# Attention of a two-layer transformer rewritten: half-array score matmuls, stacks copied inside SBUF, an unrolled order by a table

## The chip, the cores and the metric

One core of one Trainium2 chip runs the whole kernel, in one launch. The metric is the device time in microseconds, from the first to the last instruction; a comparison takes the median of several executions.

## The reference

x has 32 batches of 256 rows with 256 features, and ctx has the same shape. The network is four residual steps, each on the layer norm of x:

```python
x = x + lora_attention(layernorm(x), ctx)     # layer 0: weights W + 2*A@B, 16 heads of 16
x = x + sqrt((n @ cos(theta'))**2 + (n @ sin(phi'))**2)     # n = layernorm(x)
x = x + rope_attention(layernorm(x), ctx)     # layer 1: q, k rotated by position, 16 heads of 16
x = x + quantised_ffn(layernorm(x))           # 256 -> 1024 -> gelu -> 256
# attention: softmax(q k^T / 4) v, heads joined, times Wo, plus bo
```

Queries come from x, keys and values from ctx. All is float32.

## The kernel before, in words

`transformer` (L1302) runs five blocks one after the other: `start` (loads x, which stays in SBUF, and its statistics), `attention` for layer 0, `cos_sin_ffn`, `attention` for layer 1, and the two quantised parts. Only `attention` and a little of `start` are touched by the change.

In `attention` each engine has its own program, and semaphores tie them. The work is done by batch. Float32 accuracy is kept by splitting a number into a rounded part (HI) and the rest (LO), both of the type float32r, and adding three products: hi*hi, hi*lo, lo*hi. For a batch:

- ScalarE makes xn (L456); PE transposes xn and ctx (L307); ScalarE and VectorE take the HI and LO parts of both (L481, L487, L542).
- PE projects q and k, 12 matmuls each (L315), and v, 12 more (L324). ScalarE adds the bias and takes the HI part (L445, L449), VectorE the LO part (L547, L552). In layer 1 q and k are first rotated: VectorE shuffles rows by 8 (L560) and multiplies by the sine (L562), GpSimd multiplies by the cosine and adds (L267, L270, L280, L283).
- The parts are stored in DRAM (L195) and come back as stacks (L199): for each head, 16 rows each of HI, LO and HI of q, and HI, HI and LO of k, beside rows of zeros up to row 96. Twelve DMAs of 128 KB do this for a batch, six for each half of the heads, all issued by SyncE.
- Scores: 32 matmuls of 96 rows (L418) into `s_bank`. VectorE takes the row maxima, 16 reductions of 128x512 (L610). The negated maxima are split (L568, L570), transposed by PE (L346), copied (L575) and moved by a DMA into rows 96 and 97 of the stack of q (L204), where the stack of k has ones.
- Transposed scores: 32 matmuls of 98 rows (L429) into `t_bank`, which so already hold the score minus the maximum. ScalarE takes the exponential, 16 times 128x512 (L475).
- 64 matmul instructions give the products with v (L339); a column of ones in `vext` (L616) gives the denominators. ScalarE copies them out (L496, L511). GpSimd stores them in DRAM (L255, L287), loads the denominators (L259), stores their inverses (L274) and loads them (L276), PE spreads them over the rows (L384), GpSimd loads the products (L291), VectorE multiplies (L653), the result is split (L508, L542) and projected (L324), and VectorE adds it to x (L665); GpSimd adds bo (L263).

The order is written out by hand: `step(i, q)` has 16 slots k. In one slot PE does the scores of slot k for batch i+1 and the transposed scores of slot k for batch i, and the other pieces stand at fixed k. Batch i+2 is being prepared meanwhile and batches i-1 and i-2 are being finished. Steps 5 to 28 run in a hardware loop of two steps (`drive`), the others are written out. The buffers `qhl` and `khl` are single, and the stacks are double. The second half of a batch's stacks waits for the transposed scores of the batch two before it, since it writes the same buffer.

Of the kernel before, what the change touches and what calls it, by code (L numbers as in the profile page):

```python
# [7 lines left out]
F32 = mybir.dt.float32  # L19
# [58 lines left out]
def attention(core, layer, w, x_res, stats, extent, consts, src, scratch):  # L78

# [11 lines left out]
    with ExitStack() as ctx:  # L91
# [6 lines left out]

        qst = [sb(f"qst{j}", [98, H, S], F32R) for j in range(2)]
        kst = [sb(f"kst{j}", [98, H, S], F32R) for j in range(2)]
        prob = [sb(f"prob{j}", [P, NT, 4, S]) for j in range(2)]
        vext = [sb(f"vext{j}", [P, NT, H, SLOT]) for j in range(2)]
        whl = {n: sb(f"w{n}", [P, 2, KT, D], F32R) for n in "qkvo"}
        ctx_in = sb("ctx_in", [P, NT, D])
        xn = sb("xn", [P, NT, D])
        xT = sb("xT", [P, 2, KT, S], F32R)
        cT = sb("cT", [P, 2, KT, S], F32R)
        qhl = sb("qhl", [P, 2, KT, S], F32R)  # L110
        khl = sb("khl", [P, 2, KT, S], F32R)
        osb = sb("osb", [P, 2, 2, S])
        yd = sb("yd", [P, KT, S])

        HI, LO = (1, 0) if rope else (0, 1)
        qf, kf = (hl[:, LO, :, :].bitcast(F32) for hl in (qhl, khl))
        yhl = xT
        negm = sb("negm", [P, 2, HT, NT])
        mhl = sb("mhl", [P, 2, 2, HT * NT], F32R)
        mT = sb("mT", [2 * HT * NT, 2, P], F32R)  # L120
        den = sb("den", [P, 32])
        rden = sb("rden", [P, 32])
        rhl = sb("rhl", [P, 2, 32], F32R)
        rin = sb("rin", [2 * H, S], F32R)

        nmr, rstd = stats[:, :, 0], stats[:, :, 1]
        bqk = sb("bqk", [P, 2, KT])
        bv = sb("bv", [P, D])
        bo = sb("bo", [P, D])
        bst = sb("bst", [P, NT, 6])  # L130
        mvt = sb("mvt", [P, NT, 2])

# [1257 lines left out]
```

## Time and profile before

| what | value |
|---|---|
| runs, median of 3 | 2484.71 us (2483.47 to 2512.54) |
| profiled execution, span from first to last instruction | 2491.9 us |
| PE, VectorE, ScalarE, GpSimd busy | 78%, 70%, 53%, 32% |
| granted PE clock, mean | 0.880 of full speed |

No time other than its span is given for the profiled execution. In the profile, PE is the matmul row of TensorE and PEld its weight loads, DVE is VectorE, ACT ScalarE, POOL GpSimd, SP SyncE; a q behind a name is that engine's queue of DMA issues. L610 is line 610 of the kernel before.

### The profile page before, as it was taken

What the parts mean: (1) busy time and instruction counts of PE and PEld (TensorE: products, weight loads), DVE (VectorE), ACT (ScalarE), POOL (GpSimd) and SP (SyncE); (2) the same over time, 40 slices, a digit from 0 to 9 for tenths busy, and PEclk for the clock granted to TensorE, in tenths of its full rate; (3) what the DMA queues carried; (4) which work ended last, traced back from release to release, by engine and by line L of the source; (5) the groups of instructions that cost most, each with busy time, mean ns of one, the idle gap of its engine ahead of it and who ended that gap; (6) DMA issues with size and microseconds to landing.
All of it is one profiled execution on the core that took longest, in us unless ns stands there. A gap on an engine that the chain in (4) does not pass through costs nothing. (4 is left out here: it accounts for less than half of the span.)

```text
span 2491.9 us, 47293 instructions
## 1 busy us (share of the span) xinstructions
PE 1955.9 (78%) x14240; PEld 1576.1 (63%) x14240; DVE 1747.3 (70%) x3674; ACT 1316.8 (53%) x2381; POOL 797.0 (32%) x866
## 2 busy tenths in 40 slices
PE   1689999999999679277788777887777775786687
PEld 0567777777777467255666666666666663665676
DVE  6567778877877378465667767767666665676788
ACT  0255666656655378144444444444444443786676
POOL 3012222222222200423333333333333332221787
PEclk9899999999999689578888888888888877898899
DMA  5576887888878100356665656666666661356565
GB/s 164 107 157 145 169 172 162 166 169 166 170 161 165 53 3 0 76 104 122 123 120 116 117 109 116 119 112 118 111 118 122 121 118 54 135 220 252 196 242 186
DMA packets 259781, 333.54 MB, mean 134 GB/s; under 512 B 29152, under 2 KB 237184, under 8 KB 251520
## 3 DMA queue, kind: packets, MB, share of 16 engines
q1 hardware_dynamic: 233088, 277.00, 49.4%
q0 software_dynamic: 26624, 55.67, 9.6%
q8 instruction: 37, 0.61, 0.1%
q14 instruction: 32, 0.26, 0.0%
HBM read 185.70 MB, written 144.70 MB: 133 GB/s over the span
## 5 line engine op out<-in xcount | busy, mean ns | idle before, releaser
L610 DVE TENSOR_REDUCE L_negm<-L_s_bank 128x2 f32<-128x512 f32 x1024 | 684.4, 684 | 363.2 <-PE L_s_bank L418 360.7
L475 ACT ACTIVATE L_prob<-L_t_bank 128x512 f32<-128x512 f32 x1024 | 598.9, 598 | 631.8 <-PE L_t_bank L429 625.7
L418 PE MATMUL L_s_bank<-L_kst,L_qst 96*128 96x256 f32 x2048 | 526.1, 343 | 236.5 <-DMA L_kst<-k_scratch 176.7
L418 PEld LDWEIGHTS L_s_bank<-L_kst,L_qst 96*128 96x128 f32 x2048 | 355.4, 216 | 363.0 <-issue 142.0
L429 PE MATMUL L_t_bank<-L_qst,L_kst 98*128 98x256 f32 x2048 | 460.6, 311 | 18.3 <-ACT L_prob L475 15.2
L429 PEld LDWEIGHTS L_t_bank<-L_qst,L_kst 98*128 98x128 f32 x2048 | 361.7, 217 | 33.3 <-ACT L_prob L475 30.0
L339 PE MATMUL L_o_bank<-L_prob,L_vext 128*32 128x256 f32 x4096 | 301.1, 415 | 2.7 <-ACT L_prob L475 2.7
L1289 PE MATMUL G_acc<-G_w_out,G_hhl 128*128 128x256 f32 x1024 | 140.4, 291 | 59.4 <-DVE G_hhl L1259 59.1
L259 POOL DMA_DIRECT2D L_den<-o_scratch x64 | 35.5, 554 | 452.2 <-DMA o_scratch<-L_osb 452.2
L1289 PEld LDWEIGHTS G_acc<-G_w_out,G_hhl 128*128 128x128 f32 x1024 | 127.9, 192 | 72.1 <-DVE G_hhl L1259 37.5
L339 PEld LDWEIGHTS L_o_bank<-L_prob,L_vext 128*32 128x32 f32 x4096 | 112.5, 115 | 92.6 <-issue 18.8
L324 PE MATMUL L_m<-L_wo,L_xT 128*128 128x256 f32 x768 | 133.7, 336 | 45.0 <-DVE L_xT L542 44.9
L1219 POOL TENSOR_SCALAR G_hs<-G_hq,G_winv 128x512 f32<-128x512 f32 x128 | 152.4, 1208 | 40.8 <-issue 23.2
L324 PEld LDWEIGHTS L_m<-L_wo,L_xT 128*128 128x128 f32 x768 | 120.8, 237 | 56.2 <-DVE L_xT L542 30.9
L255 POOL DMA_DIRECT2D o_scratch<-L_osb x64 | 48.0, 751 | 301.4 <-ACT L_osb L511 301.4
L1002 PE MATMUL G_hb<-G_xT,G_w_in 128*128 128x512 f32 x512 | 127.1, 401 | 12.0 <-DVE G_xT L1112 11.2
L291 POOL DMA_DIRECT2D L_yd<-o_scratch x128 | 77.9, 614 | 140.3 <-DVE L_xT L542 130.0
L1002 PEld LDWEIGHTS G_hb<-G_xT,G_w_in 128*128 128x128 f32 x512 | 94.9, 190 | 38.0 <-ACT G_hid L1044 14.2
L1107 DVE TENSOR_REDUCE G_hmax<-G_hid 128x512 f32 (+1 forms) x128 | 84.8, 682 | 45.3 <-ACT G_hid L1044 45.3
L315 PE MATMUL L_m<-L_xT,L_wq 128*128 128x256 f32 x768 | 115.5, 304 | 1.1 <-DVE L_xT L542 1.1
L324 PE MATMUL L_m<-L_wv,L_cT 128*128 128x256 f32 x768 | 110.9, 298 | 5.9 <-ACT L_khl L445 4.1
L315 PEld LDWEIGHTS L_m<-L_xT,L_wq 128*128 128x128 f32 x768 | 108.0, 213 | 3.6 <-DVE L_xT L542 1.9
(172 smaller groups left out, 3257.2 us busy)
## 6 DMA issues: line engine op xcount, KB each, us to landing
L_qst<-q_scratch SPq DMA_DIRECT2D x384, 128.0 KB, 5.0
L_kst<-k_scratch SPq DMA_DIRECT2D x384, 128.0 KB, 6.4
q_scratch<-L_qhl SPq DMA_DIRECT2D x64, 512.0 KB, 3.0
k_scratch<-L_khl SPq DMA_DIRECT2D x64, 512.0 KB, 3.2
o_scratch<-L_osb POOLq DMA_DIRECT2D x128, 256.0 KB, 4.8
hidden_scratch<-G_hid SPq DMA_DIRECT2D x32, 1024.0 KB, 3.9
G_hid<-hidden_scratch SPq DMA_DIRECT2D x32, 1024.0 KB, 7.4
L_ctx_in<-in_ctx SPq DMA_DIRECT2D x64, 256.0 KB, 3.2
```

The costliest lines, as they stand in the source:

```text
L291: pool.dma_start(yd[:, t, :], o_dram[1 - q, t].rearrange("g (s r) q -> (g s) r q", r=SLOT)[:, 0:HD, :]).then_inc(sem["y_load"], 16)
L315: mm = pe.matmul(dst[:, f, :], wt[:, cw, k, P * f:P * (f + 1)], act[:, ca, k, :], start=j == 0, stop=j == len(group) - 1)
L324: mm = pe.matmul(dst[:, t, :], act[:, ca, k, P * t:P * (t + 1)], wt[:, cw, k, :], start=j == 0, stop=j == len(group) - 1)
L339: mm = pe.matmul(o_bank[g // 2][SLOT * s:SLOT * (s + 1), g % 2, :], vext[q][:, kt, 4 * g + s, :], prob[g % 2][:, kt, s, :], start=kt == 0, ...
L418: mm = pe.matmul(s_bank[k % 2][:, j, :], qst[1 - q][0:96, h, P * qt:P * (qt + 1)], kst[1 - q][0:96, h, :], start=True, stop=True)
L429: mm = pe.matmul(t_bank[k % 2][:, j, :], kst[q][0:98, h, P * kt:P * (kt + 1)], qst[q][0:98, h, :], start=True, stop=True)
L475: act.activation(prob[g % 2][:, k % 2, 2 * (k // 2 % 2):2 * (k // 2 % 2) + 2, :], t_bank[k % 2][:, :, :], ACT.Exp, scale=HD ** -0.5).then_ ...
L610: dve.tensor_reduce(negm[:, t, 2 * pair:2 * pair + 2, qt], s_bank[k % 2][:, :, :], AX.X, ALU.max, negate=True).then_inc(sem["dve_s"], 1)
L1002: ins = pe.matmul(hb[f % 4][:, :], w_in[:, k, P * f:P * (f + 1)], xT[q][:, c, k, :], start=j == 0, stop=j == len(group) - 1)
L1107: dve.tensor_reduce(hmax[:, bass.ds(FT * i + f, 1)], hid[q][:, f, :], AX.X, ALU.max, apply_absolute_value=True).then_inc(sem["dve_h"], 1)
L1219: pool.tensor_scalar(hs[f % 4][:, :], hq[f % 4][:, :], -MAGIC, winv[:, f:f + 1], ALU.add, ALU.mult).then_inc(sem["pool_hs"], 1)
L1289: ins = pe.matmul(acc[q][t][:, 0:D], hhl[f % 4][:, c, P * t:P * (t + 1)], w_out[:, f, :], start=f == 0 and c == 0, stop=f == FT - 1 and c ...
```

## The change

`attention` is written anew; the other three computing blocks stay.

- **Stacks.** They are copied by DMA from `qhl` and `khl` inside SBUF, not by way of DRAM: again 12 DMAs of 128 KB for a batch, in rows of 2 KB where the loads before had 1 KB. The columns of Wq and Wk are reordered on the host so that the two halves of the heads lie on even and odd partitions. The half h of batch n lies on partitions 64u to 64u+47, with u = n%2 xor h, and the maxima and ones on the two rows after that, so scores have 48 rows and transposed scores 50. In a slot the four matmuls alternate between the two halves of the array.
- **Context.** It arrives transposed. Layer 0 splits it on GpSimd and stores the parts in DRAM (512 KB a batch), and layer 1 loads them.
- **Biases.** bo + bv@Wo is computed once and comes into the output projection as one more matmul of each row tile. The bias of v, the bias additions on GpSimd and the widening products of PE go.
- **After the products.** The two groups of heads go one after the other through one PSUM tile `eo`, with 17 columns a head. ScalarE copies each out. SyncE gathers denominators (2 DMAs), merges rows (4), stores inverses (2) and loads them spread over 128 rows (1). GpSimd multiplies and takes LO.
- **Rotation.** In layer 1 four DMAs inside SBUF (two each for q and k) swap the halves, and GpSimd does all six products and sums. VectorE has none.
- **Splits.** GpSimd takes all LO parts of q, k, y and, in layer 0, of ctx, and in layer 0 the HI parts too; ScalarE takes the HI parts of layer 1. GpSimd also makes xn. All DMAs of attention are now SyncE's; GpSimd issues none.
- **Maxima.** Their split is on GpSimd in layer 1 and stays on VectorE in layer 0.
- **Order.** A table `PLACE` gives each piece a batch offset and a slot for each layer, the same in all engines, and `HELD` names whom a PSUM bank must have been read by. All steps are written out: 39 for layer 0 (offsets 4 to -3) and 43 for layer 1 (4 to -7), with no hardware loop.
- The memsets of the stacks and the mask `bmask` go.

The diff, cut to its core:

```diff
-        qst = [sb(f"qst{j}", [98, H, S], F32R) for j in range(2)]
+        qst = [sb(f"qst{j}", [P, HJ, KT, S], F32R) for j in range(2)]
...
-            with eng.Fori(2, (B - 4) // 2) as r:
-                step(2 * r + 1, 1)
-                step(2 * r + 2, 0)
+        def drive(step):
+            for i in range(start_at, end_at):
+                step(i)
...
+            def stack(n, h):
+                u = n % 2 ^ h
+                for st, hl, parts in ((kst, khl, (0, 0, 1)), (qst, qhl, (0, 1, 0))):
+                    for c, part in enumerate(parts):
+                        row = 64 * u + HD * c
+                        sp.dma_start(st[n % 2][row:row + HD, :, :, :].bitcast(F32),
+                                     hl[n % NQ][h::2, part, :, :].bitcast(F32)).then_inc(sem[f"stack{h}"], 16)
...
+                    for n in due("sti0", i, k):
+                        sp.wait_ge(sem["pool_k"], n + 1)
+                        sp.wait_ge(sem["pool_q"], n + 1)
+                        after(sp, sem["pe_t"], 16 * (n - 2) + 8)
+                        after(sp, sem["stack0"], 96 * n)
+                        stack(n, 0)
+                    for n in due("sti1", i, k):
+                        after(sp, sem["pe_t"], 16 * (n - 1))
+                        after(sp, sem["stack1"], 96 * n)
+                        stack(n, 1)
...
+            def high(n, x, hl, f):
+                pool.wait_ge(sem[f"act_{x}"], n + 1)
+                for h in range(2):
+                    after(pool, sem[f"stack{h}"], 96 * (n - NQ + 1))
+                pool.tensor_copy(hl[n % NQ][:, 0, :, :], f[:, :, :]).then_inc(sem[f"high_{x}"], 1)
...
+                        for n in due(f"ms{h}", i, k) if rope else ():
+                            pool.wait_ge(sem["dve_s"], 16 * n + 8 * (h + 1))
+                            after(pool, sem["pe_mT"], 2 * (n - 1) + h + 1)
+                            pool.tensor_copy(mhl[:, h, 0, :], negm[:, h, :]).then_inc(sem["m_split"], 1)
...
+                    first = scores(i + 1, k) if on(i + 1) else iter(())
+                    second = scores_T(i, k) if on(i) else iter(())
+                    for _ in range(KT):
+                        next(first, None)
+                        next(second, None)
```

NQ is 1. In both layers the HI and LO parts of batch n+1 can be written only after both stack copies of batch n have landed.

## Rows read from the trace of the kernel before

**Rows 1.** Windows by stage (start:end, length, busy by engine, PEclk, DMA share, GB/s)
```profile
43.00:867.60 824.60, 731.71 (x6032) 580.00 (x6032) 595.90 (x1298) 449.68 (x867) 212.29 (x294) 0.93 0.73 149
999.30:2109.00 1109.70, 832.88 (x6016) 669.60 (x6016) 737.56 (x1486) 493.32 (x930) 392.89 (x422) 0.82 0.58 111
...
300.00:700.00 400.00, 383.06 (x3327) 305.17 (x3329) 319.63 (x706) 243.64 (x476) 104.69 (x159) 0.98 0.82 167
1200.00:2000.00 800.00, 634.36 (x4651) 510.77 (x4651) 555.24 (x1135) 377.89 (x715) 284.58 (x319) 0.84 0.62 116
```
**Rows 2.** One line, L189, 300:700 and then 1200:2000: the context load, once a batch
```profile
L189 SPq DMA_DIRECT2D L_ctx_in<-in_ctx x18: 402/403/407, 312.4 to 697.6; - x18
...
L189 SPq DMA_DIRECT2D L_ctx_in<-in_ctx x24: 400/403/446, 1221.4 to 1968.7; - x24
```
**Rows 3.** Waits, 1200:1800 (us in total, times, longest)
```profile
POOL L_den L259 <- DMA o_scratch<-L_osb: 166.9, 19, 9.7
...
PE L_s_bank L418 <- DMA L_kst<-k_scratch: 78.4, 19, 5.3
```
**Rows 4.** Groups of instructions, 100:800 (layer 0)
```profile
L610 DVE TENSOR_REDUCE L_negm<-L_s_bank 128x2 f32<-128x512 f32 x485 | 321.5, 683 | 105.6 <-PE L_s_bank L418 105.4
L475 ACT ACTIVATE L_prob<-L_t_bank 128x512 f32<-128x512 f32 x479 | 279.5, 599 | 229.0 <-PE L_t_bank L429 228.0
...
L449 ACT ACTIVATE L_khl<-L_m,L_bqk 128x256 fp32r<-128x256 f32 x60 | 25.0, 473 | 0.0
...
L542 DVE TENSOR_TENSOR L_xT<-L_m,L_xT 128x512 fp32r<-128x512 f32 x30 | 20.4, 680 | 0.0
...
L665 DVE TENSOR_TENSOR x_res<-L_m,x_res 128x512 f32 (+1 forms) x27 | 18.7, 691 | 2.2 <-issue 0.4
...
L575 DVE CAST L_mT<-L_m 32x128 fp32r<-32x128 f32 x61 | 16.7, 274 | 23.9 <-PE L_m L346 23.9
...
L568 DVE CAST L_mhl<-L_negm 128x16 fp32r<-128x16 f32 x60 | 10.4, 174 | 0.2
```
**Rows 5.** Groups of instructions, 1100:2060 (layer 1)
```profile
L263 POOL TENSOR_TENSOR x_res<-x_res,L_bo 128x256 f32 (+1 forms) x58 | 41.6, 745 | 0.5
...
L283 POOL TENSOR_TENSOR L_khl<-L_khl,L_rr 128x512 f32<-128x512 f32 x29 | 37.0, 1275 | 4.2 <-POOL L_khl L280 3.8
...
L499 ACT ACTIVATE L_khl<-L_khl 128x512 fp32r<-128x512 f32 x29 | 18.3, 630 | 47.8 <-POOL L_khl L283 47.8
```
**Rows 6.** Timeline of 420 to 425: projection, score matmuls and products with v at full clock
```profile
421.65 1.49 PEld L315 LDWEIGHTS L_m<-L_xT,L_wq 128*128 128x128 f32 x12
...
423.31 0.31 PEld L429 LDWEIGHTS L_t_bank<-L_qst,L_kst 98*128 98x128 f32 x2
423.55 0.31 PEld L418 LDWEIGHTS L_s_bank<-L_kst,L_qst 96*128 96x128 f32 x2
423.79 0.31 PEld L429 LDWEIGHTS L_t_bank<-L_qst,L_kst 98*128 98x128 f32 x2
...
424.24 1.07 PE L339 MATMUL L_o_bank<-L_prob,L_vext 128*32 128x256 f32 x16
425.24 0.50 PE L418 MATMUL L_s_bank<-L_kst,L_qst 96*128 96x256 f32 x2
```
**Rows 7.** DMA issues (KB each, median us from issue to landing)
```profile
L_qst<-q_scratch SPq DMA_DIRECT2D x384, 128.0 KB, 5.0
L_kst<-k_scratch SPq DMA_DIRECT2D x384, 128.0 KB, 6.4
```
**Rows 8.** Timeline, 78 to 90: the first stacks of layer 0, with nothing beside them
```profile
82.08 1.25 SPq L199 DMA_DIRECT2D L_kst<-k_scratch  x3
...
88.40 0.80 PE L418 MATMUL L_s_bank<-L_kst,L_qst 96*128 96x256 f32 x2 [8.39 <-DMA L_kst<-k_scratch]
```
**Rows 9.** Windows, 80:90, the same stretch (columns as in rows 1)
```profile
80.00:90.00 10.00, 1.61 (x8) 1.60 (x8) 0.77 (x2) 0.00 (x0) 0.00 (x0) 0.50 1.12 164
```
**Rows 10.** Timelines, 1014 to 1060: casts on VectorE beside work on GpSimd
```profile
1018.10 3.09 DVE L535 CAST L_wo<-L_prob 128x512 fp32r<-128x512 f32 x1
...
1059.95 1.26 POOL L270 TENSOR_TENSOR L_qhl<-L_qhl,L_rr 128x512 f32<-128x512 f32 x1
...
1059.98 1.27 DVE L568 CAST L_mhl<-L_negm 128x16 fp32r<-128x16 f32 x1
```

More of the change, by code:

```diff
@@ L111, in attention @@
[L111 to L120, printed above, removed]
+        NQ = 1
+        qhl = [sb(f"qhl{j}", [P, 2, KT, S], F32R) for j in range(NQ)]
+        khl = [sb(f"khl{j}", [P, 2, KT, S], F32R) for j in range(NQ)]
@@ new lines, in attention, with on, due @@
+        block = ctx.enter_context(nc.Block())
+        place = PLACE[layer]
+        start_at, end_at = lo - max(a for a, _ in place.values()), hi - min(a for a, _ in place.values())
+        def drive(step):
+            for i in range(start_at, end_at):
+                step(i)
+        def on(n):
+            return lo <= n < hi
+        def due(op, i, k):
+            ahead, slot = place[op]
+            return [i + ahead] if slot == k and on(i + ahead) else []
+        biases = 16 * (4 if rope else 3)
@@ new lines, in scores @@
+            def scores(n, k):
+                h, j, qt = k // 8, k % 8 // 2, k % 2
+                u = n % 2 ^ h
+                if k % 8 == 0:
+                    pe.wait_ge(sem[f"stack{h}"], 96 * (n + 1))
+                after(pe, sem["dve_s"], 16 * n + k - 1)
+                rows = slice(64 * u, 64 * u + ROWS)
+                for t in range(KT):
+                    mm = pe.matmul(s_bank[k % 2][:, t, :], qst[n % 2][rows, j, t, P * qt:P * (qt + 1)], kst[n % 2][rows, j, t, :],
+                                   start=True, stop=True)
+                    if t == KT - 1:
+                        mm.then_inc(sem["pe_s"], 1)
+                    yield
@@ new lines, in scores_T @@
+            def scores_T(n, k):
+                h, j, kt = k // 8, k % 8 // 2, k % 2
+                u = n % 2 ^ h
+                if n == lo and k == 0:
+                    pe.wait_ge(sem["ones0"], 64)
+                if k % 8 == 0:
+                    pe.wait_ge(sem[f"m_load{h}"], 16 * (n + 1))
+                after(pe, sem["act_p"], 16 * n + k - 1)
+                rows = slice(64 * u, 64 * u + ROWS + 2)
+                for t in range(KT):
+                    mm = pe.matmul(t_bank[k % 2][:, t, :], kst[n % 2][rows, j, t, P * kt:P * (kt + 1)], qst[n % 2][rows, j, t, :],
+                                   start=True, stop=True)
+                    if t == KT - 1:
+                        mm.then_inc(sem["pe_t"], 1)
+                    yield
@@ L435, in _ @@
+            drive(step)
         @block.scalar
@@ L1336, in shape_constants @@
     f = np.float32
-    head = np.arange(P) // HD
-    bmask = np.zeros((2 * H, KT, P), f)
-    for t in range(KT):
-        for part in range(2):
-            bmask[part * H + HT * t + head, t, np.arange(P)] = 1
     inv_freq = f(1.0) / np.power(f(10000.0), np.arange(0, HD, 2, dtype=f) / f(HD)).astype(f)
```

886 lines of the change are left out of this document (420 added, 466 removed), and 24 rows, old and new, of tables (HELD, PLACE).

## The prediction

> **What bounds the kernel now.** I read the windows by stage first, then the interval from batch to batch, then the waits, then the groups of instructions. Attention takes 824.6 us in layer 0 and 1109.7 us in layer 1 of the 2491.9 us [rows 1]; the rest isn't touched. The context load comes once a batch. In layer 0 it came 18 times from 312.4 to 697.6 us, so 385.2/17 = 22.66 us a batch; in layer 1, 24 times from 1221.4 to 1968.7, 747.3/23 = 32.49 us a batch [rows 2]. So 32 batches make 725 us and 1040 us, and 99.6 and 69.9 us are left for filling and draining the two layers.
>
> In layer 0 PE is busy in 383 of 400 us at a clock of 0.98 [rows 1]: it is PE's layer. The DMA engines are at 0.82 there. In layer 1 PE is busy in 634 of 800 us at 0.84, and what ends its longest idle stretch in each batch is the stack of k, 78.4 us in 19 waits, up to 5.3 us [rows 3]. Layer 1 is bound by a chain: rotation, split, store, stack, with GpSimd in the middle of it and blocked in its order by the load of denominators (166.9 us in 19 waits [rows 3]).
>
> **The change part by part, for one batch.**
>
> *PE.* A pair of score matmuls starts every 0.24 us (423.31, 423.55, 423.79), so a slot of four costs 0.48 us and 16 slots 7.7 us [rows 6]. The new order alternates the two halves of the array, in 48 and 50 rows. No row here shows two such matmuls at once. If they overlap fully a slot costs 0.24 us, 3.9 us a batch; if not, 7.7 us as now. The only matmuls side by side in this trace are those of 32 columns: 16 instructions with v in 1.07 us [rows 6], where their own passes one behind the other would take several times that. I take 4.5 us. The rest of PE: four projections at 1.49 us, 6.0; two bias matmuls at 0.12, 0.25; four groups with v at 1.0, 4.0; transposes of xn and maxima about 0.8. The context's transposes and the widening go, about 1.1 us. Sum 15.6 us at full clock, 18.8 without overlap.
>
> The Trainium skill, "TensorEngine Tiling (Array Packing)", section Key Properties, says that tiles work independently but that "Changing tiling mode (not just tile) drains the TensorE". The first half speaks for the 3.9 us, the second against this change, which goes from half-array to whole-array work and back at nearly every piece. The trace has such a change: the products with v began at 424.24 and the next score matmul at 425.24 [rows 6], 1.00 us where two rounds of four fill about 0.85, so at most 0.15 us a change. With two changes in each of 12 slots that is up to 3.6 us, and PE would need 19.2 us instead of 15.6; without the rule 15.6.
>
> *VectorE.* 16 reductions at 0.683 = 10.9; LO of xT 0.68; sum with x 0.69; two copies of maxima 0.55 [rows 4]; statistics, inverse and their kin 1.3. Layer 0 adds the four small splits at 0.174, 0.7 [rows 4], layer 1 the two extents, 1.3. Sum 14.9 in layer 0 and 15.5 in layer 1, from 18.1 (0.80 of 22.66) and 22.5 (0.694 of 32.49) [rows 1, 2].
>
> A cast between SBUF tiles on VectorE takes 0.174 us alone [rows 4] and took 1.27 us while GpSimd ran a sum that ended with it, and a 128x512 cast took 3.09 us beside memsets [rows 10]. In layer 1 that cast goes to GpSimd and can no longer be held. In layer 0 it stays, twice a batch, and GpSimd will be busy for 60% of the time, so it costs 2 x 0.6 x about 0.6 = 0.7 us more, between 0 and 2.2. It delays the maxima, which have slots to spare, so I put 0.5 us of it on the interval.
>
> *ScalarE.* 16 exponentials at 0.599 = 9.6; q and k 4 x 0.473 = 1.9 [rows 4]; xT, v and two copies of eo 4 x 0.6 = 2.4. Layer 0: 13.9. Layer 1 adds three HI copies at 0.63 [rows 5]: 15.8.
>
> *GpSimd.* A sum or product of 128x512 costs 1.275 us, of 128x256 0.745 [rows 5]. A cast of 128x512 on GpSimd has no row; its bounds are 0.6, what ScalarE needs [rows 5], and 1.275; I take 1.0, nearer to GpSimd's own. Layer 0: five products at 1.275, four casts at 1.0, xn 1.2, sum 11.6. Layer 1: ten at 1.275, xn 1.2, four small splits of maxima at 0.2 to 0.4, sum 15.2. It waits in order for the gathered denominators only once a batch, at a place where the table gives them two steps.
>
> *SyncE and the DMAs.* 25 issues in layer 0 and 28 in layer 1, at 0.43 us most, 11 to 13 us. Bytes for a batch fall from about 3.7 MB (0.82 of 22.66 us = 18.6 us of all engines [rows 1, 2]) to 2.7 and 2.9 MB: 1.5 stacks, 0.25 or 0.5 context, 0.5 stored or 0.5 rotated, 0.13 merged, 0.25 inverses. At the same rate that is 13.6 and 14.6 us.
>
> *The chain that decides.* Every engine now needs 14 to 16 us, and a loop needs more. The parts of batch n+1 may be written only when both stacks of batch n have landed, the second stack may be issued only when the transposed scores of batch n-2 are through, and the first stack of n+1 must have landed at the start of the next step. So the interval is at least second stack + splits + first stack. A stack is six DMAs. In the trace three issued from 82.08 on let PE go at 88.40, 6.3 us [rows 8], in a stretch with the engines full at 164 GB/s [rows 9]; single ones land after 5.0 and 6.4 us [rows 7]. 768 KB at 164 GB/s is 4.7 us, and with 2 us of fixed latency 6.7; rows of 2 KB and no DRAM may make it 5, a last landing behind other traffic 8.6 (2.2 to issue and 6.4). I take 6.5. The splits in layer 0 are four instructions of GpSimd in a row, 4.6 us, with handoffs 5.5; in layer 1 two HI copies on ScalarE and two of 1.275 us behind them, with GpSimd at other work for three quarters of the time: 6.5. Loop: 18.5 and 19.5 us. For slots in which two engines wait for each other in turn (now too VectorE idles 105 us of 700 for PE [rows 4]) I add 1 us: **19.5 us in layer 0, 20.5 us in layer 1.**
>
> *Fill and drain.* Layer 0: 17 us to the split weights (now 24; the memsets go, beside which a cast took up to 3.09 us [rows 10]), 21 to the first scores, 13 for the step of scores alone, 31 x 19.5 = 604.5, 11 for the last exponentials, 20 to drain. Sum 686.5. Layer 1: 14 + 28 (the rotation is longer) + 13 + 31 x 20.5 = 635.5 + 11 + 22 = 723.5. The offset of -7 costs nothing: late steps hold only short work. Straight-line code instead of a loop: the loop has no visible cost and so I take 0, with -3 to +15 us in all as bounds, since 82 steps of instructions must be fetched once.
>
> *Sum.* 824.6 - 686.5 = 138.1 and 1109.7 - 723.5 = 386.2; together 524.3. 2491.9 - 524.3 = 1967.6 against the profiled span; the median of the runs is 0.9971 of it, so **1962 us**.
>
> **The rivals.**
>
> A, *PE is the bound again.* Without overlap between the halves PE needs 18.8 us, with 0.15 us at each of 24 changes of shape [rows 6] 3.6 more, 22.4, and any clock under 1 on top. Layer 0 at 22.5 and layer 1 at 23: 31 x 3 + 31 x 2.5 = 170 more, 2132 us. For it: the clock is 0.82 in layer 1 where PE is busy in 79% [rows 1], and the new kernel has PE at about 80%. Against it: with the halves overlapped 15.6/0.84 = 18.6 is still under the loop.
>
> B, *the loop is shorter.* Stacks in 5 us give 15.5 us, and the engines' 16 us with the same 1 to 1.5 on top bound it: 17 and 18. 31 x 2.5 x 2 = 155 less, 1807 us. For it: half the packets. Against it: all six copies still land on 48 partitions.
>
> C, *slower than before.* The copies inside SBUF are slow, and through the single `qhl` and `khl` the interval pays each of them twice. It decides from 523/62 = 8.4 us a batch, which is 4.2 us more for each stack, 10.7 us. At 12 us the interval is 2 x 12 + 5.5 = 29.5 in both: 31 x (10 + 9) = 589 more, 2551 us. For it: the only copy inside SBUF now, the one of maxima, is 16 KB, and single stack DMAs have 128 KB. Against it: 128 KB is landed in 5.0 to 6.4 us now, with DRAM on one side and a fuller queue [rows 7].
>
> D, *the gain is eaten elsewhere and nothing changes.* It needs the price of C at 8.4 us by chance, or SyncE's one order of 28 issues blocking itself as GpSimd's did. 2470 us.
>
> **How the numbers follow.** Forecast 0.57, A 0.17, B 0.11, C 0.11, D 0.04. The likeliest gives 1962 us. Its own range is 1900 to 2040, an interval shorter or longer by 1.2 us. The range of 8 in 10 takes in the near half of B and most of A: 1860 to 2180. About 2% is what a measurement of this kernel can tell from no change. Faster by over 2% hold the forecast, A and B, 0.85; within it D, 0.04; slower C, 0.11.
>
> **What would show it.** In the profile after: the 1024 reductions of VectorE with starts 19 to 21 us apart from batch to batch; in a slot, weight loads of the two kinds of scores side by side and slots of 0.24 to 0.3 us where nothing waits; stack DMAs landing in 4 to 6 us; GpSimd's LO of q and k ending just before SyncE issues the first stack; PE's longest wait in each step being a stack, at slot 0 or 8. GpSimd at 60% in layer 0 and 75% in layer 1. The prediction is wrong if four score matmuls still take 0.48 us and PE is busy over 90% (A), if the interval is set by VectorE with no wait for a stack (B), or if a stack needs over 10 us (C).

## The result and the profile after

| | before | after |
|---|---|---|
| median of the runs | 2488.2 us | 2364.4 us (2362.1 to 2366.3, 4 runs) |
| ratio after / before | 1 | 0.948 [0.945, 0.952] |
| span of the profiled execution | 2491.9 us | 2364.4 us |
| attention, layer 0 and layer 1 | 824.6 and 1109.7 us | 895.7 and 909.7 us |
| interval per batch, layer 0 and 1 | 22.66 and 32.49 us | 25.93 and 25.97 us |

The kernel gained 5.2%, some 124 us where 524 were forecast. Layer 1 gained 200 us; layer 0, of which 138 us were expected, lost 71. First the windows of the kernel after: the two layers whole, then the steady part of layer 0 (columns as in [rows 1]).

```profile
43.00:938.70 895.70, 693.13 (x5908) 475.76 (x5908) 454.25 (x947) 406.52 (x771) 313.15 (x361) 0.81 0.57 103
1070.40:1980.10 909.70, 707.25 (x5892) 499.07 (x5892) 464.12 (x877) 450.16 (x865) 462.53 (x521) 0.79 0.65 111
...
300.00:700.00 400.00, 311.79 (x2795) 212.86 (x2791) 209.65 (x441) 190.42 (x363) 145.79 (x166) 0.83 0.61 109
```

In that steady part PE was busy in 383 us at a clock of 0.98 before [rows 1]; now it is 312 us at 0.83. No engine and not the DMA (0.82 before, 0.61 now) is near full in it. The interval per batch, here and for every run below, is read from the issue of the spread of the inverses (`rb`), once a batch. Its rows from the middle of the two layers:

```profile
L255 SPq DMA_DIRECT2D L_rb<-r_scratch x23: 670/672/677, 223.8 to 794.2; - x23
L255 SPq DMA_DIRECT2D L_rb<-r_scratch x26: 651/672/928, 1176.4 to 1825.6; - x26
```

570.4/22 = 25.93 us, 649.2/25 = 25.97 us. The waits of the two layers (us in total, times, longest), of 300:800 and of 1200:1800:

```profile
POOL L_yT L334 <- DMA L_rb<-r_scratch: 211.5, 19, 12.8
...
ACT L_osb L552 <- POOL L_yT L334: 112.1, 19, 7.7
PE L_eo L522 <- ACT L_osb L552: 106.7, 19, 7.4
...
POOL L_khl L311 <- DMA L_qst<-L_qhl: 53.5, 19, 4.0
...
POOL L_qr L319 <- DMA L_qr<-L_qf: 143.1, 23, 7.7
POOL L_kf L319 <- DMA L_kr<-L_kf: 72.1, 23, 4.9
...
PE L_s_bank L438 <- DMA L_qst<-L_qhl: 44.6, 23, 2.9
PE L_misc L471 <- POOL L_mhl L378: 40.7, 23, 3.0
```

The first four are layer 0: PE waits not for a stack but for ScalarE's copy of `eo`, ScalarE for GpSimd's product, GpSimd for the spread. The last four are layer 1: GpSimd's two longest waits are for the rotated copies, and PE waits for a stack and for the maxima's split. The timeline of one batch of layer 0 shows the first ring (start, length; in brackets the idle time ahead and what ended it):

```profile
417.56 0.57 SPq L228 DMA_DIRECT2D L_den<-L_osb  x1
419.33 1.91 SPq L217 DMA_DIRECT2D L_kst<-L_khl  x3
...
421.10 0.34 DVE L642 RECIPROCAL L_rden<-L_den 128x32 f32<-128x32 f32 x1
421.28 1.89 SPq L217 DMA_DIRECT2D L_qst<-L_qhl  x3
423.27 1.14 SPq L251 DMA_DIRECT2D r_scratch<-L_rden  x2
...
425.69 3.84 SPq L246 DMA_DIRECT2D L_osb<-L_osb  x4
429.63 0.68 SPq L255 DMA_DIRECT2D L_rb<-r_scratch  x1
430.40 1.88 SPq L217 DMA_DIRECT2D L_kst<-L_khl  x3
...
437.44 1.26 POOL L334 TENSOR_TENSOR L_yT<-L_osb,L_rb 128x512 f32<-128x512 f32 x1 [12.43 <-DMA L_rb<-r_scratch]
438.79 0.60 ACT L552 ACTIVATE L_osb<-L_eo 128x512 f32<-128x512 f32 x1 [7.38 <-POOL L_yT L334]
...
439.53 1.91 PE L522 MATMUL L_eo<-L_prob,L_vext 128*17 128x256 f32 x16 [7.11 <-ACT L_osb L552]
...
440.78 0.61 POOL L311 CAST L_khl<-L_kf 128x512 fp32r<-128x512 f32 x1 [2.08 <-DMA L_qst<-L_qhl]
```

The denominators leave at 417.56 and are inverted at 421.10; the inverses are stored only at 423.27, 1.8 us after they are ready, because a stack's six issues stand ahead in SyncE's order; the spread goes out at 429.63, behind four merges, and GpSimd's wait for it ends 7.8 us later, beside the next stack. Only then may GpSimd multiply and ScalarE copy the next half into the single `osb`, for which PE waits. The stack issued from 430.40 on is whole only when GpSimd can begin the next splits, at 440.78, 10.4 us later. All 25 issues of a batch of layer 0 share SyncE's one order.

The terms that had been forecast stand in the groups of layer 0 (300:700), the DMA issues, and one slot at full clock:

```profile
L622 DVE TENSOR_REDUCE L_negm<-L_s_bank 128x2 f32<-128x512 f32 x244 | 160.4, 683 | 185.0 <-PE L_s_bank L438 183.1
...
L311 POOL CAST L_qhl<-L_qf 128x512 fp32r<-128x512 f32 x15 | 9.2, 613 | 0.0
```
```profile
L_kst<-L_khl SPq DMA_DIRECT2D x384, 128.0 KB, 4.6
L_qst<-L_qhl SPq DMA_DIRECT2D x384, 128.0 KB, 5.3
...
L_qr<-L_qf SPq DMA_DIRECT2D x64, 128.0 KB, 4.8
L_kr<-L_kf SPq DMA_DIRECT2D x64, 128.0 KB, 6.8
```
```profile
406.98 0.28 PE L438 MATMUL L_s_bank<-L_kst,L_qst 48*128 48x256 f32 x1
...
406.98 0.28 PE L454 MATMUL L_t_bank<-L_qst,L_kst 50*128 50x256 f32 x1
...
407.21 0.28 PE L438 MATMUL L_s_bank<-L_kst,L_qst 48*128 48x256 f32 x1
```

Both kinds of score matmuls start at the same hundredth of a microsecond, and two pairs, which make a slot, take 0.23 us (406.98 to 407.21). That is the price where slots follow each other. Many stand between pieces of whole-array work, as here in the kernel after, and then, for comparison, the start of the score matmuls behind the projection of [rows 6] in the kernel before:

```profile
417.70 0.98 PE L427 MATMUL L_misc<-L_wv,L_cT 128*128 128x256 f32 x6
...
418.61 0.38 PE L438 MATMUL L_s_bank<-L_kst,L_qst 48*128 48x256 f32 x1
...
419.04 0.98 PE L427 MATMUL L_misc<-L_wv,L_cT 128*128 128x256 f32 x6
```
```profile
423.07 0.31 PEld L418 LDWEIGHTS L_s_bank<-L_kst,L_qst 96*128 96x128 f32 x2
```

Six whole-array matmuls and one slot of two pairs take 1.34 us (417.70 to 419.04), where eight passes at 0.115 us would take 0.92: each of the two changes between whole-array and half-array work costs 0.2 us. The matmul records of 300:700 hold some 20 such changes a batch, 4 us by that price (an estimate). In the kernel before, the twelve weight loads from 421.65 on and the first of the scores at 423.07 are 0.118 us apart, so that change cost nothing.

### The profile page after: what moved, and what is told of

Read it like the earlier page. It is cut to its first block and busy times, and to the rows that moved or that the text cites. A ratio compares the mean times of both kernels' runs of the same rounds, so it can differ in the third digit from the quotient of the medians.

```text
span 2364.4 us, 41257 instructions
## 1 busy us (share of the span) xinstructions
PE 1792.0 (76%) x13992; PEld 1301.9 (55%) x13992; DVE 1332.9 (56%) x2715; ACT 1230.9 (52%) x2221; POOL 969.2 (41%) x1032
## 5 line engine op out<-in xcount | busy, mean ns | idle before, releaser
L438 PE MATMUL L_s_bank<-L_kst,L_qst 48*128 48x256 f32 x2048 | 495.0, 354 | 74.5 <-DMA L_qst<-L_qhl 65.9
L454 PE MATMUL L_t_bank<-L_qst,L_kst 50*128 50x256 f32 x2048 | 485.1, 352 | 43.4 <-DMA L_qst<-L_mT 33.6
L438 PEld LDWEIGHTS L_s_bank<-L_kst,L_qst 48*128 48x128 f32 x2048 | 336.6, 217 | 264.6 <-issue 95.6
L522 PE MATMUL L_eo<-L_prob,L_vext 128*17 128x256 f32 x4096 | 351.4, 480 | 164.5 <-ACT L_osb L552 164.5
L454 PEld LDWEIGHTS L_t_bank<-L_qst,L_kst 50*128 50x128 f32 x2048 | 334.6, 218 | 61.0 <-DMA L_qst<-L_mT 42.8
L427 PE MATMUL L_misc<-L_wo,L_yhl 128*128 128x256 f32 x768 | 135.4, 322 | 0.0
L420 PE MATMUL L_misc<-L_xT,L_wq 128*128 128x256 f32 x768 | 130.5, 309 | 2.1 <-DVE L_xT L637 2.1
L427 PE MATMUL L_misc<-L_wv,L_cT 128*128 128x256 f32 x768 | 130.9, 311 | 0.9 <-ACT L_qf L538 0.9
L420 PE MATMUL L_misc<-L_cT,L_wk 128*128 128x256 f32 x768 | 122.2, 305 | 4.3 <-POOL L_cT L348 4.3
L427 PEld LDWEIGHTS L_misc<-L_wo,L_yhl 128*128 128x128 f32 x768 | 124.6, 233 | 0.0
```

Source lines behind the costliest of these rows:

```text
L420: mm = pe.matmul(bank[x][:, f, :], whl[x][:, cw, k, P * f:P * (f + 1)], act[:, ca, k, :], start=j == 0, stop=j == 5)
L427: mm = pe.matmul(bank[x][:, t, :], act[:, ca, k, P * t:P * (t + 1)], whl[x][:, cw, k, :], start=j == 0 and x != "o", stop=j == 5)
L438: mm = pe.matmul(s_bank[k % 2][:, t, :], qst[n % 2][rows, j, t, P * qt:P * (qt + 1)], kst[n % 2][rows, j, t, :], start=True, stop=True)
L454: mm = pe.matmul(t_bank[k % 2][:, t, :], kst[n % 2][rows, j, t, P * kt:P * (kt + 1)], qst[n % 2][rows, j, t, :], start=True, stop=True)
L522: mm = pe.matmul(eo[SLOT * j:SLOT * j + VS, t, :], vext[n % 3][:, kt, VS * head:VS * (head + 1)], prob[h][:, kt, j, t, :], start=kt == 0, ...
```

## The experiments

Intervals in us per batch, each read over the first 28 of a layer's 31 intervals; the last three, where the layer drains, are mostly 15 to 21 us and are left out. The ratio is to the kernel before, with its 95% interval.

| run | median us | ratio | layer 0 | layer 1 |
|---|---|---|---|---|
| after | 2364.4 | 0.948 [0.945, 0.952] | 26.0 | 26.0 |
| f1_osb2 | 2317.3 | 0.929 [0.926, 0.932] | 24.6 | 26.3 |
| f2_nq2 | 2357.6 | 0.947 [0.944, 0.950] | 25.7 | 26.2 |
| g1_osb2_nq2 | 2236.2 | 0.898 [0.895, 0.900] | 21.9 | 26.0 |
| f3_order0 | 2419.6 | 0.972 [0.969, 0.975] | 27.7 | 25.9 |
| h2_both_order0 | 2419.4 | 0.970 [0.966, 0.974] | 28.1 | 26.1 |
| h1_cut_loops | 2227.4 | 0.893 [0.890, 0.896] | 21.7 | 26.2 |
| h3_no_merge | 2306.5 | 0.926 [0.922, 0.930] | 24.5 | 25.6 |
| g2_act_queue | 2429.1 | 0.976 [0.974, 0.979] | 24.5 | 29.3 |
| g3_osb2_nq2_actq | 2403.3 | 0.964 [0.961, 0.967] | 24.0 | 29.2 |
| i1_pool_merge | 2384.6 | 0.958 [0.954, 0.963] | 20.6 | 32.2 |
| f4_ms_dve | 2360.7 | 0.947 [0.945, 0.950] | 25.8 | 26.3 |
| i2_bufs_ms_dve | 2227.4 | 0.896 [0.892, 0.901] | 21.6 | 26.1 |
| g4_apart | 2361.9 | 0.949 [0.945, 0.953] | 25.8 | 26.1 |
| i3_small_third | 2255.2 | 0.907 [0.904, 0.911] | 25.2 | 23.0 |
| j2_bufs_small_third | 2120.3 | 0.850 [0.847, 0.853] | 20.9 | 23.2 |
| j1_best | 2213.7 | 0.889 [0.885, 0.892] | 20.5 | 26.4 |

Kernels that have the same code in a layer differ by up to 0.4 us there, so less than that shows nothing. Some of the recorded texts below put the kernel with both buffers at 24.2 to 25 us in layer 1, and i3 at 3.5 us less than the kernel after: those were read over other stretches, some with draining batches in them. Read alike, layer 1 stands at 26.3 us with `osb` doubled (28 intervals from 1133.9 to 1869.9) and at 26.0 with both buffers (1058.8 to 1786.1).

### The two single buffers

```diff
-        osb = sb("osb", [P, 2, KT, S])
+        osbs = [sb(f"osb{j}", [P, 2, KT, S]) for j in range(2)]   # f1, g1: osbs[n % 2]
...
-                            after(act, sem["pool_y"], n)
+                            after(act, sem["pool_y"], n - 1)
...
-        NQ = 1
+        NQ = 1 if rope else 2                                     # f2, g1
```

f1_osb2:

> osb is doubled in both layers, so the copy of eo for batch n+1 no longer waits for the product of batch n; nothing else moves. Theory T1 (in layer 0 the loop through the single osb binds: copy of eo, denominators, inverses, their spreading, product, next copy): PE's 7 us stall before the products with v goes, and the interval of layer 0 falls from 25.9 to 20 to 22 us, layer 1 stays: 2190 to 2260 us. Theory T2 (the loop of the prediction, through the single qhl and khl, binds, now with SyncE's issues in it): the stall moves to the stacks and the interval stays at 25 to 26 us: 2340 to 2365 us.

f2_nq2:

> qhl and khl are doubled in layer 0 alone. T1: no change, 2355 to 2370 us. T2: the interval of layer 0 falls by the splits and the landing that leave the loop, 3 us or more: 2270 us or less.

g1_osb2_nq2:

> osb doubled in both layers and qhl/khl doubled in layer 0, that is the two buffers of the two earlier runs together. Theory of two loops (copy of eo, inverses, product; and splits, first stack, second stack, each closed by one single buffer): alone the doubled osb left 24.6 us a batch of layer 0 and the doubled qhl/khl 25.7; together neither loop is left there, the batch falls to what the engines and issues want, 19 to 21 us, so 2317 - 32 x 4.6 = about 2170 us (2120 to 2220). Rival, that SyncE's one order of issues with its waits carries the interval whatever the buffers: 24 to 24.6 us a batch, 2300 to 2320 us. Layer 1 at 26.0 in both.

Alone the doubled `osb` brought 47 us, and the doubled parts 7, with layer 0's interval at 25.7; together they brought 128. In f1 PE's waits for the copy of `eo` went, but the ring of splits and stacks held. One lap of it, from f1's timelines of SyncE, PE and GpSimd:

```profile
404.95 1.90 SPq L218 DMA_DIRECT2D L_kst<-L_khl  x3
...
413.35 0.38 PE L439 MATMUL L_s_bank<-L_kst,L_qst 48*128 48x256 f32 x1 [0.54 <-DMA L_qst<-L_qhl]
...
414.66 1.87 SPq L218 DMA_DIRECT2D L_kst<-L_khl  x3
...
426.20 0.61 POOL L312 CAST L_khl<-L_kf 128x512 fp32r<-128x512 f32 x1 [3.48 <-DMA L_qst<-L_qhl]
...
429.90 1.88 SPq L218 DMA_DIRECT2D L_kst<-L_khl  x3
```

The first stack is issued from 404.95 on, and PE waits for it until 413.35, 8.4 us. The second is issued 9.7 us after the first, and GpSimd's splits wait for it until 426.20, 11.5 us. The splits take 3.7 us, and the next first stack leaves at 429.90: 9.7 + 11.5 + 3.7 = 24.9 us in this lap, for a mean of 24.6. So two rings of nearly one length lay beside each other in layer 0, and only cutting both pays: 26.0 to 21.9 us. Of the 19 to 21 us expected g1 kept 0.9 more than the upper end, and its time is 16 us outside the range given. Layer 1 stayed at 26 us, as expected.

### Where the issues stand in SyncE's order

```diff
-     "sti0": (3, 5), "mg": (0, 9), "rs": (0, 6), "rb": (0, 10)    # layer 0: f3, and h2 on g1
+     "sti0": (3, 6), "mg": (0, 5), "rs": (0, 5), "rb": (0, 6)
...
-     "ym": (-1, 8)                                                # layer 0: h1 on g1
+     "ym": (-2, 2)
...
-     "kr": (1, 3)                                                 # layer 1: h1 on g1
+     "kr": (2, 14)
```

f3_order0:

> Layer 0's table only: merging, storing and spreading of the inverses are issued by SyncE before the first stack of the next batch, not behind it. T1: the product starts 6 to 8 us earlier after the copy of eo, and the interval falls to about 20 us until the stack, issued later, binds: 2170 to 2250 us. T2: the first stack comes later, and the interval grows or stays: 2360 us or more.

h2_both_order0:

> The kernel with both buffers, and layer 0's table as in the earlier run of another order (merges, store of the inverses and spread ahead of the first stack), which alone cost 55 us. Theory: alone it delayed the splits' ring, which was closed by the single qhl/khl; with two of each it cuts the ring through the spread instead (store, merges and spread no longer wait for the stack), so the same edit now saves: 19 to 20.5 us a batch for 21.4, 2160 to 2215 us. Rival, that an earlier place of these issues is simply bad (they block SyncE until the inverses are ready): slower than 2236 here too, by 20 to 60 us.

h1_cut_loops:

> The kernel with both buffers (2236 us), and one step moved in each layer. Layer 0 (21.4 us a batch there): GpSimd's product with the spread inverses goes behind the splits of k and q, so the splits, and with them the first stack and all that SyncE issues behind it, no longer wait for the spread (spread 7.5 us, product and splits 5.0, stack 3.8, store, merges and the next spread 5.1 = 21.4). Theory that this ring through SyncE's and GpSimd's orders sets the interval: 17 to 19.5 us a batch, 32 x 3 = about 100 us less. Layer 1 (24.2 us there): the rotated copies of k are issued ahead of the spread and the load of c, 1.4 to 2 us earlier in the ring rotated copies, rotation, splits, first stack, rotated copies: 22.5 us a batch, 40 to 60 us less. So about 2090 us (2050 to 2140). Rival, DMA or TensorE near their bound (TensorE 16 to 17 us, DMA 14): layer 0 stays at 20.5 or above and the total at 2180 or more.

Putting the inverses ahead of the first stack cost 55 us alone and 183 us where both buffers are doubled, against the 20 to 75 us of gain that I expected there. The waits of h2_both_order0, layer 0 (265:800), and its timeline say why:

```profile
PE L_s_bank L439 <- DMA L_qst<-L_qhl: 134.4, 20, 9.4
```
```profile
414.22 0.60 ACT L553 ACTIVATE L_osb<-L_eo 128x512 f32<-128x512 f32 x1 [0.39 <-PE L_eo L523]
...
420.97 0.65 SPq L256 DMA_DIRECT2D L_rb<-r_scratch  x1
421.79 1.86 SPq L218 DMA_DIRECT2D L_kst<-L_khl  x3
```

The next stack is issued only behind the store and the spread, which wait for the present batch's copy, which waits for its matmuls: scores, products, inverses and the next stack are in one line, and PE stands for it up to 9.4 us a batch. An issue that waits for the end of the present batch must not stand ahead of one that feeds the next.

h1 moved GpSimd's product behind the splits. The splits no longer waited for the spread, but the interval stayed at 21.7 us; in layer 1, where the rotated copies of k were issued earlier, it stayed at 26.2, and 2227 is 9 us from g1, with 100 to 190 expected. The ring that I had read off g1's timeline (spread, product, splits, stack, store, merges, spread) was thus not the only one of its length; which one holds the 22 us isn't settled.

### Taking issues out of the order

```diff
-                        for g in range(4):       # all five runs; h3 has nothing in its place
-                            sp.dma_start(osb[32 * g + HD:32 * (g + 1), 0, :, :], osb[32 * g:32 * g + HD, 1, :, :]).then_inc(sem["merge"], 16)
...
+                            act.dma_start(den[64 * h:64 * (h + 1), :], osb[HD:P:32, h, :, :]).then_inc(sem[f"den_load{h}"], 16)   # g2, g3: behind each copy of eo
+                            if h == 1:           # and then the four merges
+                                for g in range(4):
+                                    act.dma_start(osb[32 * g + HD:32 * (g + 1), 0, :, :], osb[32 * g:32 * g + HD, 1, :, :]).then_inc(sem["merge"], 16)
...
+                        for g in range(4):       # i1, and j1 in layer 0 alone: ahead of the product
+                            pool.dma_start(osbs[n % 2][32 * g + HD:32 * (g + 1), 0, :, :], osbs[n % 2][32 * g:32 * g + HD, 1, :, :]).then_inc(sem["merge"], 16)
```

h3_no_merge:

> Kernel after without the four merges a batch: the odd heads' values aren't moved into the tile that is multiplied, 4 of SyncE's 25 to 28 issues go and nothing else. They take 2.5 us a batch of issuing, 3.8 us with their wait in layer 0. Theory that SyncE's one order lies in the rings that set the interval in both layers: 2.5 to 3.8 us a batch less in layer 0, 1.5 to 2.5 in layer 1, 130 to 200 us less than 2364: about 2200 us. Rival, issues are cheap and the rings are made of landings alone: within 40 us of 2364.

g2_act_queue:

> Kernel after, but ScalarE issues the two loads of the denominators and the four merges right behind its copies of eo, in both layers; 6 of SyncE's 25 to 28 issues a batch leave its order. Theory that SyncE's one order lies in both loops: in layer 0 the four merges (3.8 us) go from between the inverses' store and their spread, the first loop falls to some 22 us and the second, which has 6 issues less to wait behind, to 24 or below: 24 us a batch for 25.9, 2364 - 60 = about 2300 us, more if layer 1 (26.0) gains as well (2240 to 2330). Rival, that ScalarE's own order pays it back (six issues of 0.6 us and the wait for the first load in front of the exponentials): 2360 to 2420 us.

g3_osb2_nq2_actq:

> The two before together: osb doubled, qhl/khl doubled in layer 0, denominators and merges issued by ScalarE. If buffers alone carry the interval this is as the run with both buffers (within 20 us). If SyncE's order does, it is the first kernel that falls clearly in layer 0: 19 to 21 us a batch, and 23 to 25 for 26.0 in layer 1, so 2317 - 32 x 4.6 - 32 x 2 = about 2105 us (2050 to 2170).

i1_pool_merge:

> The kernel with both buffers (2236 us), with the four merges a batch issued by GpSimd right ahead of its product, in both layers. SyncE issues for 16 to 17 of 21.5 us a batch there in layer 0 and for 17 of 24 in layer 1; the merges are 2.5 to 3.3 of it. Theory that SyncE's order is near its own bound: layer 0 at 19 to 20.5 us, layer 1 at 22 to 24, 2130 to 2190 us. Rival, GpSimd's issues cost it more than SyncE's and stand ahead of its splits and products: 2250 us or more.

j1_best:

> The kernel with both buffers (2236 us), with GpSimd issuing the merges in layer 0 alone. In the run with them on GpSimd in both layers, layer 0 stood at 20.3 us a batch for 21.7, layer 1 at 32.2 for 25. If the layers are independent: 32 x 1.4 = 45 us less than 2236, 2190 us (2175 to 2210). Rival, that the gain in layer 0 was chance of its placing: 2236 within 15 us.

Without the merges layer 0 falls by 1.5 us a batch and layer 1 by 0.4, in all 58 us, less than the 130 to 200 expected: the 2.5 us of issuing lie only partly in the rings. On ScalarE the same issues cost more than they free. Timeline of g2_act_queue:

```profile
430.36 0.59 ACTq L542 DMA_DIRECT2D L_den<-L_osb  x1
431.05 2.50 ACTq L547 DMA_DIRECT2D L_osb<-L_osb  x4
...
434.24 0.38 PE L441 MATMUL L_t_bank<-L_qst,L_kst 50*128 50x256 f32 x1 [2.70 <-ACT L_prob L534]
```

Five issues take 3.2 us of ScalarE's order at one point, where exponentials stand behind them and PE behind those (2.7 us here); layer 0 still gains 1.5 us, layer 1 loses 3.3. With both buffers doubled as well (g3) the layers stand at 24.0 and 29.2 us and the kernel is 167 us slower than g1, where one theory had it at g1's time and the other at 2105 us: with the rings cut, the issues on ScalarE cost 2.1 us a batch in layer 0 and 3.2 in layer 1. Among i1's rows are the issue and the landing of the merges from GpSimd (timeline, then DMA issues), and the window of 300:700, in layer 0 (columns as in [rows 1]):

```profile
424.43 2.00 POOL L330 DMA_DIRECT2D L_osb<-L_osb  x4
```
```profile
L_osb<-L_osb POOLq DMA_DIRECT2D x256, 32.0 KB, 4.0
```
```profile
300.00:700.00 400.00, 371.24 (x3587) 264.30 (x3590) 283.76 (x566) 244.94 (x470) 222.03 (x289) 0.94 0.81 139
```

GpSimd issues four in 2.0 us and they land after 4.0 us, where SyncE's took 2.5 us and landed after 2.0. In layer 0 GpSimd stands idle there anyway: 20.6 us, 1.2 less than g1. PE is then busy in 371 of 400 us at a mean clock of 0.94, 19.1 of the 20.6 us of a batch: it is nearly the bound again, as it was before. In layer 1, where GpSimd has ten products a batch and the rotation waits behind the merges, it is 32.2 us, 6 more. j1_best uses GpSimd's issues in layer 0 alone: 20.5 and 26.4 us, 2213.7 us, 22 below g1 where 45 were expected, and the fastest kernel here that computes everything. Its layer 0 gave the gain, 40 us from the first spread to the last; its layer 1, with g1's code, took 14 us more, which isn't explained.

### The maxima's split

```diff
-                        for n in due(f"ms{h}", i, k) if rope else ():     # on GpSimd
+                        for n in ():
...
-                        for n in due(f"ms{h}", i, k) if not rope else (): # on VectorE
+                        for n in due(f"ms{h}", i, k):                     # at (1, 7) and (1, 15)
```

f4_ms_dve:

> The split of the maxima goes back to VectorE in layer 1, right behind the last reduction of each half; all else as in the changed kernel. If GpSimd's order (its wait for the rotated q stands ahead of the split) holds the second maxima of each batch, PE's 1.7 us wait for them a batch goes and the interval of layer 1 falls by 1.5 to 3 us: 2270 to 2320 us. If the cast is held by GpSimd's own work as before (up to 1.27 us, twice a batch) as much as it gains, or the stacks bind, the time stays: 2350 to 2375 us.

i2_bufs_ms_dve:

> The kernel with both buffers (2236 us), with layer 1's split of the maxima back on VectorE and at the earlier kernel's places. On kernel after alone this changed nothing. There TensorE waits for GpSimd's split 35 us in 22 steps of layer 1 (1.6 us a batch). If that wait lies in what sets the 24 us, 32 x 1.6 = some 50 us less: 2185 us (2160 to 2210); if it lies beside the ring of the rotated copies and the splits on GpSimd, as before: 2236 within 15 us.

Neither changed the time measurably: 3.6 us less on the kernel after, 9 less on g1, with layer 1 at 26.3 and 26.1 us for 26.0. PE's 41 us of waiting for that split [the waits above] lie beside a ring that is as long without them.

### The halves of the array

```diff
-                    for _ in range(KT):
-                        next(first, None)
-                        next(second, None)
+                    for part in (first, second):
+                        for _ in range(KT):
+                            next(part, None)
```

g4_apart:

> Kernel after, but the eight score matmuls of a slot are issued four of one kind and then four of the other, so the halves of the array do not run beside each other: some 0.45 us more of TensorE a slot, 7 us a batch, or 3 us by the pitch of 0.24 a pair seen before. TensorE's own work goes from about 16 to 19 to 23 us a batch. Theory that loops outside TensorE hold 25.9 and 26.0 us: below those all the same, so 2360 to 2400 us. Rival, that TensorE is part of the loops (the products wait in its order behind the scores): 2450 to 2560 us.

2361.9 us, no change. But the edit didn't do what it was to do. Timeline of g4_apart:

```profile
418.08 0.28 PE L438 MATMUL L_s_bank<-L_kst,L_qst 48*128 48x256 f32 x1
418.09 0.28 PE L454 MATMUL L_t_bank<-L_qst,L_kst 50*128 50x256 f32 x1
418.20 0.28 PE L438 MATMUL L_s_bank<-L_kst,L_qst 48*128 48x256 f32 x1
```

In PE's program both matmuls of one kind now stand ahead of both of the other (two of each a slot, where the text on record counts four), and they still start in pairs 0.11 us apart. So the run doesn't say what PE costs without overlap. That PE isn't the bound of the kernel after is shown by i1 and j1, in which the same matmuls fit in 20.6 us a batch.

### The bytes of the stacks

In i3 and j2 the scores' third terms are old for 224 of 256 columns from the third batch on.

```diff
+                        m = 32 if c == 2 and n >= lo + 2 else S
-                        sp.dma_start(st[n % 2][row:row + HD, :, :, :].bitcast(F32),
-                                     hl[n % NQ][h::2, part, :, :].bitcast(F32)).then_inc(sem[f"stack{h}"], 16)
+                        sp.dma_start(st[n % 2][row:row + HD, :, :, 0:m].bitcast(F32),
+                                     hl[n % NQ][h::2, part, :, 0:m].bitcast(F32)).then_inc(sem[f"stack{h}"], 16)
```

i3_small_third:

> Kernel after with every issue in its place, but from the third batch of each layer on the third of each stack's three copies moves only 32 of 256 columns (the third terms of the split scores are then left from earlier batches for the rest): 0.29 of the stacks' bytes go, 0.45 MB of 1.5 MB a batch. Theory of the orders and issues: the stacks' bytes matter little, 25 to 26 us a batch stays, 2310 to 2364 us. Rival, the stacks' bytes and the queue they make carry the interval (landings of 4.6 to 5.3 us fall to 3.5): two stacks a ring, 2 to 3 us a batch in both layers, 2364 - 64 x 2.5 = about 2205 us (2170 to 2250).

j2_bufs_small_third:

> The kernel with both buffers, with the third of each stack's copies cut to 32 of 256 columns from the third batch on (its terms of the scores are then old for the rest). On kernel after this brought 0.6 us a batch in layer 0 (held there by the ring through the single osb) and 3.5 in layer 1. Theory that with the rings cut the stacks' bytes count in layer 0 too: 21.6 to 19 or 20 us there, 22.5 in layer 1: 2236 - 32 x 2 - 32 x 2.5 = about 2090 us (2050 to 2130). Rival, that SyncE's 16 us of issues and their order hold layer 0: 21 us there, 2150 us or more in all.

All issues stay. On the kernel after this brought 109 us, most of it in layer 1: 26.0 to 23.0 us, and 26.0 to 25.2 in layer 0. Neither theory was right for both layers. The DMA issues of i3_small_third:

```profile
L_kst<-L_khl SPq DMA_DIRECT2D x264, 128.0 KB, 3.8
L_qst<-L_qhl SPq DMA_DIRECT2D x264, 128.0 KB, 4.3
...
L_qr<-L_qf SPq DMA_DIRECT2D x64, 128.0 KB, 2.9
L_kr<-L_kf SPq DMA_DIRECT2D x64, 128.0 KB, 5.5
```

With fewer stack bytes the rotated copies land after 2.9 and 5.5 us for 4.8 and 6.8, and a stack copy 0.8 to 1.0 us sooner. Where layer 0's rings are cut first (j2), the interval there goes from 21.9 to 20.9 us, in layer 1 from 26.0 to 23.2, and it is 116 us in all.

## Why the prediction was wrong

The step that failed is "The chain that decides": it took 6.5 us for a stack, which took 8.4 to 11.5, and it counted one ring of DMAs and waits where a second one, as long, lay beside it, both lengthened by SyncE's one order of issues. Term by term:

- **Direction, layer 1.** Right: the chain through DRAM and GpSimd's blocked order went, 32.5 to 26.0 us a batch.
- **PE.** Not the bound, but the term was too small. I took 4.5 us a batch for the scores, between 3.9 with full overlap and 7.7 without. The halves do run beside each other: two pairs take 0.23 us where four matmuls took 0.48 before [rows 6], 3.7 us a batch where slots follow each other. But a change between half-array and whole-array work costs 0.2 us (1.34 us for eight passes, above), more than my "at most 0.15 us", and the sum of 15.6 us had it at nothing. By the Trainium skill, "TensorEngine Tiling (Array Packing)", section Key Properties, a change of mode drains the array; the trace agrees that a change costs time. Part of the 0.2 us may be a weight load that is no longer hidden behind a matmul, since the first score matmul after a change is recorded with 0.38 us (418.61) and the others with 0.28; the rows can't part the two. My 0.15 was read up to the start of that record, and its "two rounds of four" were four rounds. In i1's layer 0 PE was busy for 19.1 us a batch, close to the 19.2 that I had worked out with the rule. So even without the rest an interval of 19.5 us would have stood close to what PE needs.
- **VectorE, ScalarE.** Reductions took 0.683 us, as before. VectorE was busy in 56% and ScalarE in 52% of the span; neither held an interval.
- **GpSimd.** The cast was mis-sized, 0.61 us and not 1.0, in the safe direction, and GpSimd was busy in 35% of layer 0 and 51% of layer 1, not in 60% and 75%. The 0.5 us for VectorE's held cast was announced and then left out of the loop's sum. The step "It waits in order for the gathered denominators only once a batch, at a place where the table gives them two steps" failed: in layer 0 GpSimd stands 11 us a batch for the spread (211.5/19), and ScalarE's copy and PE's products stand behind it.
- **SyncE.** "25 issues in layer 0 and 28 in layer 1, at 0.43 us most" failed. Three of a stack's copies take 1.9 us to issue, 0.63 each; from 419.33 to 445.26 of layer 0 the issues fill 15 to 16.5 us, not 11. Worse than the sum is their order: I had put this blocking into rival D, at 0.04.
- **The stacks.** "I take 6.5" failed. Single copies inside SBUF land after 4.6 and 5.3 us, no later than the loads before, but a stack is six of them, and from its first issue to its last landing the trace of layer 0 has a median of 8.2 us for the first stack of a batch and 10.3 for the second; 10.4 us stands in the timeline above, and 8.4 and 11.5 in f1's lap. Issuing the six takes 3.8 us of it, and everything else lands beside them: the spread after 7.8 us, the rotated copies after 4.8 and 6.8. I had taken the figure from a stretch in which three issues let PE go [rows 8]. By the landings in the same trace, the six loads of a half took 8.9 and 9.2 us in the steady part of layer 0 before. i3 shows that 3 us of layer 1's interval hang on the bytes.
- **The deciding chain.** "So the interval is at least second stack + splits + first stack" was true and named only one ring, at 19.5 and 20.5 us: 6.5 + 5.5 + 6.5 and 1 more. In f1, where it holds, its parts are 9.7, 3.7 and 11.5 us. The second stack is issued 9.7 us after the first, not 6.5, because SyncE issues other things between the two, and it takes 11.5 us to be there; the splits were shorter than forecast. And I had missed the ring through the single `osb` (copy, denominators, inverses, spread, product, next copy), 25.9 us. Had I walked the chain behind the products as I walked the one ahead of the scores, with its issues in the table's order, the stack's six issues would have stood in it. Before, the output's DMAs were issued by GpSimd (L255, L259), and SyncE had 17 a batch, none of which waited for the products; that is the likely reason why layer 0 became slower, though no run put them back. In layer 1 GpSimd waits longest for the rotated copies, issued between two stacks, and its six products stand behind them; I had only given the splits 1 us more for it. That these make the chain of layer 1 is read from the waits: no run cut it, and issuing one pair of them earlier (h1) changed nothing.
- **Fill and drain.** 895.7 - 32 x 25.93 = 66 us and 909.7 - 32 x 25.97 = 79 us, for 62.5 and 67.5 in my sums. So nearly the whole miss of 397 us on the profiled span is the interval: 32 x (6.4 + 5.5) = 381.
- **Rivals.** A and B didn't occur; A's price for the changes of shape did, without setting the interval. C's sign, a stack of over 10 us, came for the second stack of each batch, and its mechanism, slower stacks that the interval pays for through the single `qhl` and `khl`, is part of what happened; it cost less than C had, since the first stack took 8.2 us and layer 1 gained. D's blocking of SyncE's one order is another part, but with layer 1's gain the two left 2364 and not 2470 us.

## What to carry to other kernels

Before a forecast by "the loop", list every buffer that exists once, and walk each one's ring with all its DMAs in the order in which the one queue issues them; the interval is the longest ring, and cutting one of two equal rings shows almost nothing. Moving DMAs to one idle-looking engine makes its order a shared resource: never put an issue that waits for the end of this batch ahead of one that feeds the next, and give issues to another engine only where nothing critical stands behind them. A DMA's landing must be read with the traffic that the new order puts beside it, and a set of DMAs from its first issue to its last landing, in the loaded part of the trace.

## What the runs showed of the hardware

- Two kinds of matmuls on different rows of the array start together even when both of one kind stand ahead of both of the other in the program (418.08 and 418.09 in g4_apart).
- Going from whole-array to half-array matmuls or back cost 0.2 us each time (1.34 us for six and two passes from 417.70 on), and going between 128 and 96 rows in the kernel before nothing.
- Six copies of 128 KB inside SBUF, issued in 3.8 us, were all there after 8.4 to 11.5 us in f1's lap, where a single one lands after 4.6 or 5.3 us.
- A copy of 128 KB inside SBUF in rows of 2 KB costs SyncE 0.63 us to issue; the context load from DRAM costs 0.40. The merges (32 KB) cost SyncE and ScalarE 0.62 each, and GpSimd 0.50, but GpSimd's land after 4.0 us instead of 2.0.
- The mean granted clock was 0.83 in the steady part of layer 0 of the kernel after, with PE busy in 78%, 0.94 in i1 with 93%, and 0.98 before with 96% [rows 1]. Over the whole span it was 0.831 in the kernel after and 0.879 in j2_bufs_small_third.
- GpSimd's wait for the spread of 256 KB ended 7.8 us after its issue when a stack was issued right behind it.
